# Adding the value bias on TensorE and copying the values out of PSUM in eight pieces, in a four-layer attention and feed-forward kernel

## The reference

```python
Q = (q @ wq.T + bq).reshape(b, s, H, DK).transpose(0, 2, 1, 3)
K = (k @ wk.T + bk).reshape(b, -1, H, DK).transpose(0, 2, 1, 3)
V = (v @ wv.T + bv).reshape(b, -1, H, DK).transpose(0, 2, 1, 3)
```

## Time and profile before

| what | value |
|---|---|
| median of the runs | 1589.87 us |
| the profiled execution's own time | 1589.54 us |
| span of that execution, first to last instruction | 1587.7 us |
| instructions | 22618 |
| TensorE clock granted, mean | 0.832 of full speed |
| busy over the span: TensorE, VectorE, ScalarE | 1205.8 us (76%), 1010.5 us (64%), 612.6 us (39%) |
| routing stage, from the slots to the next stage | 673 to 729 us of the span |
| preparation stage of layer 3 | 1377 to 1401 us of the span |

### The profile page before, as it was taken

The page is one execution under the profiler, slowest core; times in us unless marked ns, Lnnn a source line. Parts: engine busy times, 40 slices in busy tenths (PEclk is TensorE's granted clock), DMA queues, the critical chain, the costliest instruction groups (busy, mean ns, idle before and its releaser), DMA issues. The chain is left out here.

```text
span 1587.7 us, 22618 instructions
## 1 busy us (share of the span) xinstructions
PE 1205.8 (76%) x6805; PEld 878.8 (55%) x6805; DVE 1010.5 (64%) x3444; ACT 612.6 (39%) x1154; POOL 256.2 (16%) x240
## 2 busy tenths in 40 slices
PE   4788799999866652235926886999999999758862
PEld 2656589899744452113614554677777777425531
DVE  7778746666648859833357775565556665446768
ACT  3475434444332231011224651444444444336631
POOL 1334001001001000071474320000000000023401
PEclk9899889999965555566955996999999999769985
DMA  7342100000000040312224310000000000024301
GB/s 232 104 122 67 29 1 1 2 0 0 1 1 1 0 161 15 106 46 82 79 77 111 105 50 1 1 1 1 1 1 0 0 1 1 1 67 125 97 7 53
DMA packets 54757, 69.43 MB, mean 44 GB/s; under 512 B 6784, under 2 KB 35712, under 8 KB 54016
## 3 DMA queue, kind: packets, MB, share of 16 engines
q1 hardware_dynamic: 51328, 61.78, 13.5%
q0 software_dynamic: 3328, 6.43, 1.3%
HBM read 44.99 MB, written 23.59 MB: 43 GB/s over the span
## 5 line engine op out<-in xcount | busy, mean ns | idle before, releaser
L781 POOL TENSOR_TENSOR mha_ks<-KS,w_ctx 104x1024 fp32r<-104x1024 f32 (+1 forms) x48 | 90.9, 1895 | 681.8 <-POOLq L100 497.5
L2275 DVE SCALAR_TENSOR_TENSOR tree_hl<-tree_pH,tree_hh 128x512 fp32r<-128x512 f32 x192 | 132.4, 690 | 94.9 <-ACT tree_hh L2172 93.0
L2172 ACT ACTIVATE tree_hh<-tree_pH 128x512 fp32r<-128x512 f32 x192 | 114.6, 597 | 146.2 <-PE tree_pH L2076 146.2
L833 DVE TENSOR_REDUCE mha_nm<-mha_pS 128x16 f32<-128x1024 f32 x96 | 117.2, 1221 | 22.7 <-PE mha_pS L603 19.7
L1423 ACT ACTIVATE ffn_hid<-ffn_pH,w_ffn 128x512 f32<-128x512 f32 x128 | 85.5, 688 | 55.2 <-PE ffn_pH L1346 54.6
L2089 PE MATMUL tree_pY<-tree_hh,w2h 128*128 128x512 f32 x192 | 100.9, 525 | 4.8 <-DVE tree_hl L2275 4.7
L724 ACT ACTIVATE XH<-mha_pST 128x1024 f32<-128x1024 f32 x96 | 97.8, 1019 | 11.6 <-PE mha_pST L624 11.0
L603 PE MATMUL mha_pS<-mha_ks,mha_qs 96*128 96x256 f32 (+1 forms) x384 | 80.5, 337 | 25.8 <-DVE mha_nm L833 16.7
L1535 DVE SCALAR_TENSOR_TENSOR ffn_acc<-ffn_pE,ffn_wt,ffn_acc 128x128 f32<-128x128 f32 x192 | 54.0, 345 | 68.9 <-PE ffn_pE L1359 68.9
L1359 PEld LDWEIGHTS ffn_pE<-W2R,ffn_hid 128*128 128x128 f32 x768 | 94.6, 194 | 4.4 <-issue 0.2
L1359 PE MATMUL ffn_pE<-W2R,ffn_hid 128*128 128x128 f32 x768 | 95.2, 278 | 0.0
(11 more groups left out here) (476 smaller groups left out, 2779.0 us busy)
## 6 DMA issues: line engine op xcount, KB each, us to landing
mha_qs<-queries SPq DMA_DIRECT2D x72, 256.0 KB, 4.2
queries<-mha_qh SPq DMA_DIRECT2D x24, 256.0 KB, 2.1
queries<-mha_ql SPq DMA_DIRECT2D x24, 256.0 KB, 2.4
EW<-in_L_W_dram SPq DMA_DIRECT2D x32, 128.0 KB, 2.7
EW<-in_tree_full_dram SPq DMA_DIRECT2D x2, 1536.0 KB, 8.2
slots_in<-route_zero SPq DMA_DIRECT2D x4, 640.0 KB, 11.5
X<-in_x_dram SPq DMA_DIRECT2D x8, 256.0 KB, 7.2
exp_xe<-slots_in SPq DMA_DIRECT2D x16, 128.0 KB, 2.1
```

The lines of the kernel that those rows point to most:

```text
L781: pool.tensor_tensor(ks[b % KB][0:K1, :, :, :], kb, hb, ALU.mult).then_inc(s["k"], 1)
L833: dve.tensor_reduce(nm[:, t, :], pS[:], AX.X, ALU.max, negate=True).then_inc(s["nm"], 1)
L2172: act.activation(hh[k % 2][:], pH[k % 2][:], ACT.Relu).then_inc(s["h"], 1)
L2275: dve.scalar_tensor_tensor(hl[k % 2][:], pH[k % 2][:], 0.0, hh[k % 2][:], ALU.max, ALU.subtract).then_inc(s["lo"], 1)
```

## The change

`prep_parts` gets a number `on_act`, the count of value banks that ScalarE copies; it is 4 in the routing stage and 2 in the two others. Where there is a bias, TensorE first multiplies a row of 128 ones by the row of the bias into the value's place in PSUM, and the value product adds to it. The values then leave PSUM by plain copies, two for each bank: all eight by ScalarE in the routing stage, four by ScalarE and four by VectorE in the stage of layer 3. The 32 sums of each stage go. The ones come with the first pack, which is 128 columns wider. For layer 0 the instructions stay as they are.

```diff
         for b in range(B):
-            pe.matmul(pv[b // 4][:, P * (b % 4):P * (b % 4) + P], c2[:, b, :, :], w("wv"), start=True, stop=True).then_inc(s_v, 1)
+            to = pv[b // 4][:, P * (b % 4):P * (b % 4) + P]
+            if not key_mask:
+                pe.matmul(to, core.w("ctx", "one")[0:1, :], w("bv")[0:1, :], start=True, stop=False)
+            pe.matmul(to, c2[:, b, :, :], w("wv"), start=key_mask, stop=True).then_inc(s_v, 1)
...
-        if key_mask:
-            for n in range(2):
+        if not key_mask:
+            act.wait_ge(s_z, 2)
+        for n in range(on_act):
                 act.wait_ge(s_v, 4 * n + 4)
                 for h in range(2):
                     q = slice(64 * h, 64 * h + 64)
...
-        dve.wait_ge(s_z, 2)
-        bv = w("bv").rearrange("p (c h d) -> p c h d", h=2, d=HD)
-        for h in range(2):
-            q = slice(64 * h, 64 * h + 64)
-            dve.memset(VB[q, :, :, 2 * HD + h:2 * HD + h + 1], 1.0)
-            for n in range(4):
-                dve.wait_ge(s_v, 4 * n + 4)
-                src = values_of(pv[n], q, h)
-                dst = VB[q, 4 * n:4 * n + 4, :, h * HD:h * HD + HD]
-                for bb in range(4):
-                    dve.tensor_tensor(dst[:, bb], src[:, bb], bv[q, :, h, :], ALU.add)
+        if not key_mask:
+            dve.wait_ge(s_z, 2)
+            for h in range(2):
+                dve.memset(VB[64 * h:64 * h + 64, :, :, 2 * HD + h:2 * HD + h + 1], 1.0)
+        for n in range(on_act, 4):
+            dve.wait_ge(s_v, 4 * n + 4)
+            for h in range(2):
+                q = slice(64 * h, 64 * h + 64)
+                dve.tensor_copy(VB[q, 4 * n:4 * n + 4, :, h * HD:h * HD + HD], values_of(pv[n], q, h))
...
-        prep = prep_parts(core, 2, False, st, [pX[0][:], pX[1][:]], [pL[:], pM[:], pP[:], pR[:]])
+        prep = prep_parts(core, 2, False, st, [pX[0][:], pX[1][:]], [pL[:], pM[:], pP[:], pR[:]], on_act=4)
...
-    out["ctx"] = [("ident", np.eye(P, dtype=np.float32)),
+    out["ctx"] = [("one", np.ones((1, P), np.float32)), ("ident", np.eye(P, dtype=np.float32)),
```

More of the change, by code:

```diff
@@ L167, in values_of, with prep_parts @@
     return bank[q, :].rearrange("p (b c h d) -> p b c h d", b=4, h=2, d=HD)[:, :, :, h, :]
-def prep_parts(core, L, key_mask, st, pk, pv, between=None):
+def prep_parts(core, L, key_mask, st, pk, pv, between=None, on_act=2):
     KS, VB = core.KS[L], core.VB[L]
@@ L221, in on_vector @@
                     between(dve, NQ * n + g)
-        if key_mask:
-            for n in range(2, 4):
-                dve.wait_ge(s_v, 4 * n + 4)
-                for h in range(2):
-                    q = slice(64 * h, 64 * h + 64)
-                    dve.tensor_copy(VB[q, 4 * n:4 * n + 4, :, h * HD:h * HD + HD], values_of(pv[n], q, h))
-            return
-        dve.wait_ge(s_z, 2)
-        bv = w("bv").rearrange("p (c h d) -> p c h d", h=2, d=HD)
-        for h in range(2):
-            q = slice(64 * h, 64 * h + 64)
-            dve.memset(VB[q, :, :, 2 * HD + h:2 * HD + h + 1], 1.0)
-            for n in range(4):
-                dve.wait_ge(s_v, 4 * n + 4)
-                src = values_of(pv[n], q, h)
-                dst = VB[q, 4 * n:4 * n + 4, :, h * HD:h * HD + HD]
-                for bb in range(4):
-                    dve.tensor_tensor(dst[:, bb], src[:, bb], bv[q, :, h, :], ALU.add)
+        if not key_mask:
[7 more added lines that the diff above has]
+                dve.tensor_copy(VB[q, 4 * n:4 * n + 4, :, h * HD:h * HD + HD], values_of(pv[n], q, h))
     return on_tensor, on_scalar, on_vector
```

## The result

The changed kernel is slower: a median of 1598.83 us over 20 runs (1592.19 to 1606.13) against 1588.75 us of the kernel before on the same chips (20 runs, 1580.88 to 1591.91). The ratio is 1.0068 with an interval of 1.0055 to 1.0081. The forecast was 1586.5 in a range of 1578.4 to 1589.2, so it was wrong in sign. The profiled execution took 1597.87 us with a span of 1596.0, 8.3 more than before, at a mean granted clock of 0.827.

The account below looks back on a forecast made before the run. It took the kernel as stages each ended by their slowest engine, VectorE in the two changed ones; -4.6 routing, +1.1 layer 3 and +0.2 load make -3.3, so a median of 1586.5 us, range 1578.4 to 1589.2.

Parts of the forecast that it names:

- Layer 3's stage, +1.1: Preparation of layer 3: 32 sums leave VectorE, but 64 product records end later and the last copies follow, +1.1 us.
- I take the value products' own pace: Layer 3's stage: added one-row products cost 0.1115 us a record like value products, so 64 records take 7.3 us.
- upper bound of +1.6: Layer 3's stage: at the 6-row products' 1.15 us for eight records, the added products cost 0.5 us more.
- Rival D: Layer 3's products run at half clock, 0.213 us a record: +7.7 us in place of +1.1, 1593.2 us; chance 6%.
- TensorE is now active for longer: Layer 3's stage: argument that the clock stays full through the products, as it had before; no size given.
- Routing stage, -4.6: Routing stage: sums go, late counts stay until 719.2, then 5.01 us of masks; end at 724.2 instead of 728.84.
- this is covered by the wait: Routing stage: 32 more TensorE records at 0.11 us end at about 697, hidden by the wait until 719.2.
- neither of the two places: Routing-stage sign: the first mask's wait ends as late counts or their absence predict (next stage near 724.5, or 716 to 717.5).
- Rival B: Routing stage: late counts go, so the scatter ends the stage, -12.8 us there; -11.0 in all, 1578.9 us; chance 20%.
- Rival C: Routing stage: VectorE's own counts are late too, end at 725.1, -2.5 us in all, 1587.4 us; chance 12%.
- POOL beside the masks, 0 to 0.5: Routing stage: VectorE's mask steps beside POOL's issues cost 0 to 0.5 us each, taken as nothing in the likeliest case.
- Load, +0.2: Load at the start: the first pack grows by 65.5 KB and SP's queue is held back, +0.2 us.

Follow-up runs that it names:

- 128 rows: The changed kernel with the bias product over 128 rows (all but one zeros) in place of one row: 1585.24 us, ratio 0.9989.
- 64 rows: The changed kernel with the bias product over 64 rows (63 of them zeros) in place of one: 1598.42 us in one run.
- the fold with the changed order: The fold with two banks' value products between key products, mask transposes before the rest, ScalarE copying three banks in layer 3: 1576.67 us, ratio 0.9926.
- The fold: The changed kernel without bias products, the value bias carried once through the output weights into the output bias: 1582.32 us, ratio 0.9958.

## Why the prediction was wrong

**Layer 3's stage, +1.1: the step that failed.** It read "I take the value products' own pace, as the eight records differ only by their first", with 64 records in 7.3 us at full clock. The run took 20.68 us and the stage grew by 15.2. By the experiments this is 1.5 for 64 records at the value products' pace (128 rows; against 1.1, so the rest of the step was sized rightly), 6.2 for the changes of row count (64 rows), and 7.5 that go with the half clock (one row). The nearest row taken for the bound, products over 6 rows, stood among their own kind, and so could not show what a neighbour with 128 rows costs. Its upper bound of +1.6 was too low by 13.6. That a one-row product has the pace of a full one holds, as the kernel with all bias products first shows; what fails is the step from there to a mixed row of products.

**Rival D, 6%.** It had the direction and part of the mechanism: the clock went to half within the products. Its price of +7.7 lacked the changes of rows. Its 0.213 us a record doesn't follow from the row beside it, where eight in 2.07 with a last one of 0.42 give 0.236; value products at half clock in the fold with the changed order do show it (eight from 694.73 to the next group's start at 696.43, 1.70 / 8). "TensorE is now active for longer" was the argument against it; the trace after has TensorE without a gap from 1388.30 on and the clock falls at 1391.7. The stretch ahead of the products was read as half clock, though its row has 0.66. In layer 3's stage the clock fell within the run of all three kernels with one-row products (3.4, 1.6 and 5.7 us in), and with 64 or 128 rows it held throughout. Yet in the routing stage it held through 8.8 us with one wide one-row product a bank, so one-row products don't bring it down each time. What does isn't settled by these runs.

**Routing stage, -4.6.** The mechanism stands: late counts stay until some 46 us behind the slots, the first mask is released there, and 5 us of masks follow. The fold shows it, -4.6. The term that failed is "this is covered by the wait": 32 more records were given a cover of 22 us at 0.11 us each. They needed far more, since beside the scatter TensorE's records slow to one in 0.7 us or more after some 40 in a row, in which the kernel before with its 32 just fitted. It is nearer to a count than to a time: 40 records in 4.6 us with 128 rows, 42 in 8.8 with 64, 46 in 12.9 with one. The last product ended at 49.4 instead of 24 behind the slots, and the stage gained 1.1. That the first mask's wait ended at neither of the two places was named beforehand as a sign that the reading is wrong.

**Rival B, 20%.** It didn't come: counts stay late with twice the records, with a quarter of the updates and with none of the added products. It was also priced too high. Its floor set the stage's end at 0.27 us behind the last DMA traffic (716.0), whereas the end of a scatter-bound stage is 4.34 behind the last issue: 46.1 behind the slots, a gain of 9.9 rather than 12.8.

**Rival C, 12%.** VectorE's first mask step came through to TensorE in time in the kernel with one bias product a bank (transpose at 697.23, beside the scatter), so VectorE's counts aren't late.

**POOL beside the masks, 0 to 0.5.** In the fold with the changed order one issue took 1.67 us in place of 0.97 beside the 1.15 us step on the second mask, and in the kernel with the later scatter one took 2.07 beside the same step. That is 0.70 and 1.10 more, above the stated range. In the first of them the scatter's last issue ended 42.29 behind the slots, and not 41.66 as in the kernel after, beside whose scatter only the small first steps stood. The reduction behind it (2.29 us) left issues at 0.97. The Trainium skill, page "SBUF — State Buffer", section "SBUF: two separate sides", warns that a VectorE operation which takes the shared ports keeps GpSimd from writing the descriptors of its DMAs. The traces agree for that one step.

**Load, +0.2.** The stage behind it starts at 12.87 where it started at 12.98: no cost.

## What to carry to other kernels

Price an added matmul by its neighbours, not by itself: here each change of the number of rows between neighbours cost 0.2 us at full clock, and every added product made two, beside the 0.22 us of its own; padding the operand to 128 rows took that away. Work added under a wait is free only if the engine can get through it in that time, so look at what bounds the engine there and not at the length of the wait alone. A bias that is constant over a softmax's rows is better moved out of the loop (folded, -0.4%) than to another engine.

## What the runs showed of the hardware

- A change in the number of rows between neighbouring matmuls costs 0.196 us at full clock (64 against 128 rows; with one row a product starts every 0.41 us too); at half clock a product starts every 0.72 us in place of the 0.43 that two records of 0.213 take, 0.29 more. The weight load behind a change shows an idle gap of 0.22 us at half clock, and in unmixed runs there is none.
- One-row products among themselves have the normal pace (14 records in 1.56 us). In layer 3's stage the granted clock fell from 1.00 to 0.50 within each of the three runs that held them, and in neither of those with 64 or 128 rows; but it stayed at 1.00 through a routing run of 8.8 us that held them too. What decides it is open.
- Beside 32 indirect DMAs issued by POOL, TensorE's records past the first 40 or so come one in 0.70 us or a multiple of it, and its counts come up to some 25 us late. Both end some 4.3 us behind the last issue, 3.2 behind the last traffic. A later start of the scatter took it all away. The trace after has no packet of an instruction queue from 673 to 728 us, which speaks against a wait for instructions that a DMA brings in that stretch. What holds TensorE there otherwise wasn't tried and is open.
